# Cross-attention and quantized feed-forward: value-block loads issued in parts, some softmax-side work and the first key and query products in another order

## The reference

```python
q = (layernorm(x) @ Wq); k = context @ Wk; v = context @ Wv      # 8 heads of 64
attn = softmax(einsum('bhsd,bhld->bhsl', q, k) * scale)
x = x + (einsum('bhsl,bhld->bhsd', attn, v) -> rows) @ Wo + bo
xq = fake_quant(layernorm(x))        # one scale from the largest |value| of the whole tensor
h = fake_quant(silu(xq @ qw(w_gate).T) * (xq @ qw(w_up).T))     # again one scale for all of h
x = x + h @ qw(w_down).T
```

## Time and profile before

| | us |
|---|---|
| median of 3 runs | 533.98 (533.91 to 534.53) |
| the profiled execution | 534.28 |
| its span | 532.5 |
| TensorE busy in the span | 523.9 |
| VectorE busy | 448.7 |

### The profile page before, as it was taken

The page is one execution under the profiler, slowest core; times in us unless marked ns, Lnnn a source line. Parts: engine busy times, 40 slices in busy tenths (PEclk is TensorE's granted clock), DMA queues, the critical chain, the costliest instruction groups (busy, mean ns, idle before and its releaser), DMA issues.

```text
span 532.5 us, 7840 instructions
## 1 busy us (share of the span) xinstructions
PE 523.9 (98%) x2659; PEld 352.8 (66%) x2666; DVE 448.7 (84%) x808; ACT 288.9 (54%) x416; POOL 229.4 (43%) x347
## 2 busy tenths in 40 slices
PE   8999999999999999999999999999999999999997
PEld 8888788787888888888777644444444445444444
DVE  4968798989989899898899689998999988776663
ACT  4844645565465654554435745545554543999300
POOL 4397679688596886866454000000000000055332
PEclk9999999999999999999999999999999999999999
DMA  8946365846667566435959984842243021499997
GB/s 307 315 180 183 112 180 187 285 155 211 221 196 245 182 224 190 153 111 169 224 84 353 247 207 180 319 120 44 77 118 94 26 41 30 163 334 209 135 111 127
DMA packets 82941, 93.81 MB, mean 176 GB/s; under 512 B 47085, under 2 KB 50157, under 8 KB 82645
## 3 DMA queue, kind: packets, MB, share of 16 engines
q1 hardware_dynamic: 77877, 84.13, 51.5%
q0 software_dynamic: 4320, 7.87, 9.9%
q10 hardware_dynamic: 704, 1.31, 0.8%
HBM read 47.51 MB, written 37.78 MB: 160 GB/s over the span
## 4 chain that ended last, share of the span: by engine, by line
PE 91%; DVE 4%; DMA 2%; issue 1%; SPq 1%; ACT 1%; POOL 0%; DVEq 0%
PE SP L653 14%; PE QO L648 14%; PE SP L450 6%; PE QO L415 4%; PE QO L414 4%; PE QO L413 4%; PE SP L693 4%; PE PTP L693 4%; PE QO L693 4%; PE PTP L483 3%; PE WOP L523 2%; PE WOP L525 2%; PE WOP L524 2%; PE MI L525 2%; PE MI L523 2%; PE MI L524 2%
## 5 line engine op out<-in xcount | busy, mean ns | idle before, releaser
L1599 POOL DMA_DIRECT2D out<-n2b x30 | 28.0, 974 | 204.6 <-DVE n2b L1410 204.5
L936 ACT ACTIVATE sil<-QO,fsc 128x512 f32<-128x512 f32 x87 | 59.8, 687 | 72.2 <-PE QO L648 71.3
L648 PE MATMUL QO<-nT,wgu 128*128 128x512 bf16 x340 | 87.2, 379 | 0.0
L653 PE MATMUL SP<-nT,wgu 128*128 128x512 bf16 x340 | 87.2, 379 | 0.0
L1357 DVE SCALAR_TENSOR_TENSOR h<-SP,fsc,sil 128x512 f32<-128x512 f32 x87 | 65.3, 750 | 16.1 <-PE SP L653 14.1
L1492 POOL TENSOR_TENSOR PN<-P,rs 128x512 f32<-128x512 f32 x64 | 44.6, 719 | 41.6 <-DVE rs L1019 41.6
L1363 DVE TENSOR_REDUCE hmx<-h 128x1 f32<-128x512 f32 x88 | 59.9, 685 | 2.9
L653 PEld LDWEIGHTS SP<-nT,wgu 128*128 128x128 bf16 x340 | 33.3, 98 | 40.1
L648 PEld LDWEIGHTS QO<-nT,wgu 128*128 128x128 bf16 x340 | 33.3, 98 | 40.1
L758 ACT ACTIVATE P<-P,r 128x616 f32<-128x616 f32 x32 | 25.9, 811 | 52.6 <-DVE P L1010 52.6
L965 ACT ACTIVATE h<-h,g 128x1536 int8<-128x1536 f32 (+2 forms) x38 | 44.3, 1262 | 0.0
(11 more groups left out here) (256 smaller groups left out, 1199.7 us busy)
## 6 DMA issues: line engine op xcount, KB each, us to landing
xTr<-in_xT SPq DMA_DIRECT2D x8, 1024.0 KB, 7.2
xn<-in_x SPq DMA_DIRECT2D x32, 256.0 KB, 4.0
out<-x SPq DMA_DIRECT2D x32, 256.0 KB, 3.1
n_rows<-n SPq DMA_DIRECT2D x32, 256.0 KB, 2.9
n2b<-n_rows SPq DMA_DIRECT2D x32, 256.0 KB, 3.6
out<-n2b POOLq DMA_DIRECT2D x30, 256.0 KB, 5.6
h_spill<-h SPq DMA_DIRECT2D x2, 2816.0 KB, 8.6
h<-h_spill SPq DMA_DIRECT2D x6, 768.0 KB, 8.0
```

The source lines that it names most:

```text
L648: mm = e.matmul(QO[:, at:at + 512], wgu_v[:, k, cols(ic)], nT[:, b % 2, :, k, :], start=(k == 0), stop=(k == 3))
L653: mm = e.matmul(SP[:, at:at + 512], wgu_v[:, k, cols(NI + ic)], nT[:, b % 2, :, k, :], start=(k == 0), stop=(k == 3))
L936: e.activation(sil[:, n % SR, :], QO[:, (n % 2) * 512:(n % 2) * 512 + 512], ACT.Silu, scale=fsc[:, ic:ic + 1]).then_inc(silu, 1)
```

## The change

Four things are changed; every operation stays, and the arithmetic too.

- *The start.* The second chunks of keys and Wk are requested ahead of Wq. TensorE does `k_chunk(1)` before the sums of Wq; the eighth key bank's nine products stand together behind chunk 2 (`k_last`). The first two query products run side by side in two banks, 24 matmuls in a fixed order, each with a wait for the one half it needs. ScalarE alternates wqs and xTs halves with three key copies between; both query copies come ahead of the halves of Wv. The low half of Wk's third chunk moves from VectorE to GpSimd.
- *Behind the value products.* On ScalarE `PV_high` comes ahead of `normed` (block 1: of `w_round(2)`), and normed(22) behind PT_high(28). On VectorE `second_stats`/`second_aggr` of tile 4b-5 stand behind soft_sub; the statistics of tiles 5 and 6 are moved to two other places. `split_hi` stands ahead of `w_round(4b+1)`.
- *The requests.* `load_vb` is parted: the 4 large requests stay, of the 8 small ones 4 stand in the turn of tile 4b+1 and 4 in that of 4b+2, behind `store_n2`.
- *The end.* `load_n2(0)` is requested behind store_n2(25), three stores earlier; store_v(0) ahead of load_w(0).

```diff
@@ -370,42 +370,77 @@
...
+                if k < 2:
+                    w.wait_ge(wk_lo, k + 1)
+                else:
+                    w.wait_ge(wk_lo_pool, 1)
+                for m in range(7):
                     mm = k_part(m, k, 1)
                     if k == 2:
                         mm.then_inc(k_mm, 1)
+            def k_last():
+                w.wait_ge(wq_c, 4)
+                for k in range(3):
+                    for i in (0, 2, 1):
+                        mm = k_part(7, k, i)
+                mm.then_inc(k_mm, 1)
...
+                pairs = [q_pairs(0), q_pairs(1)]
+                banks = [qo_bank("q", 0, 0), qo_bank("q", 0, 1)]
+                def high(m, k):
+                    w.wait_ge(wq_hi, k + 1)
+                    w.wait_ge(xT_hi, k + 1)
+                    return e.matmul(banks[m], pairs[m][k][0], pairs[m][k][2], start=(k == 0), stop=False)
...
+                high(0, 0)
+                weight_low(0, 0)
+                input_low(0, 0)
+                high(0, 1)
+                w.wait_ge(K_act, 3)
+                w.wait_ge(K_dve, 1)
+                high(1, 0)
+                weight_low(1, 0)
+                input_low(1, 0)
+                high(1, 1)
+                for m in range(2):
+                    weight_low(m, 1)
+                for m in range(2):
+                    high(m, 2)
+                for m in range(2):
+                    input_low(m, 1)
+                for m in range(2):
+                    high(m, 3)
+                weight_low(0, 2)
+                input_low(0, 2)
+                weight_low(0, 3)
+                input_low(0, 3).then_inc(q_mm, 1)
+                weight_low(1, 2)
+                input_low(1, 2)
+                weight_low(1, 3)
+                input_low(1, 3).then_inc(q_mm, 1)
@@ -534,12 +569,13 @@
             k_chunk(0)
+            k_chunk(1)
             w.wait_ge(ws_sum, 3)
             e.matmul(WOP[:, :], ones[:, :], wsum[0], start=True, stop=True).then_inc(wq_sum, 1)
-            k_chunk(1)
             k_chunk(2)
+            k_last()
             q_first()
-            for m in range(1, 4):
+            for m in range(2, 4):
                 q_chunk(0, m)
@@ -789,28 +825,30 @@
             e.dma_start(wkr[:, 0, :], wk_v[0]).then_inc(ld_k[0], 16)
+            e.dma_start(wkr[:, 1, :], wk_v[1]).then_inc(ld_k[1], 16)
             e.dma_start(wqr[:, 2:4, :], wq_v[:, 2:4, :]).then_inc(ld_wq, 16)
-            e.dma_start(wkr[:, 1, :], wk_v[1]).then_inc(ld_k[1], 16)
             e.dma_start(wkr[:, 2, :], wk_v[2]).then_inc(ld_k[2], 16)
+                if k == 2:
+                    k_out(0, 0)
+                    k_out(0, 1)
+                    k_out(1, 0)
                 w.wait_ge(wq_c, k + 1)
                 copy(wqs[:, 0, k, :], wqr[:, k, :]).then_inc(wq_hi, 1)
-            for k in range(4):
                 split_hi(0, k)
-            k_out(0, 0)
-            k_out(0, 1)
-            for m in range(1, 8):
+            for m in range(2, 8):
                 k_out(m, 0)
+            q_copy(0, 0)
+            q_copy(0, 1)
             for k in range(3):
                 w.wait_ge(ld_wv, 16)
                 copy(wvs[:, 0, k, :], wvr[:, k, :]).then_inc(wv_hi, 1)
-            q_copy(0, 0)
+            q_copy(0, 2)
             w.wait_ge(ld_wo, 16)
             copy(wos[:, 0], wor[:, :, :]).then_inc(wo_hi, 1)
-            for m in range(1, 4):
-                q_copy(0, m)
+            q_copy(0, 3)
@@ -842,12 +880,13 @@
-            w_round(2)
             for b in range(1, 7):
                 s = 4 * b
+                PV_high(b - 1)
                 if b > 1:
                     normed(s - 6)
-                PV_high(b - 1)
+                else:
+                    w_round(2)
                 PT_high(s)
@@ -863,11 +902,11 @@
                 q_copy(b + 1, 3)
-                if s + 1 < 26:
-                    w_round(s + 1)
                 if b + 2 < NB:
                     for k in range(4):
                         split_hi(b + 2, k)
+                if s + 1 < 26:
+                    w_round(s + 1)
                 PT_high(s + 2)
@@ -877,9 +916,9 @@
                 normed(s - 3)
-            normed(22)
             PV_high(6)
             PT_high(28)
+            normed(22)
             soft_exp(29)
@@ -1100,23 +1141,24 @@
             split_k(0)
+            split_k(1)
             w.wait_ge(ld_wq, 32)
             e.tensor_tensor(wsum[0], wqr[:, 0, :], wqr[:, 1, :], ALU.add).then_inc(ws_sum, 1)
             e.tensor_tensor(wsum[1], wqr[:, 2, :], wqr[:, 3, :], ALU.add).then_inc(ws_sum, 1)
             w.wait_ge(ws_sum, 2)
             e.tensor_tensor(wsum[0], wsum[0], wsum[1], ALU.add).then_inc(ws_sum, 1)
-            split_k(1)
+            split_k(2)
             for k in range(4):
                 w.wait_ge(wq_sum, 1)
                 e.scalar_tensor_tensor(out=wqr[:, k, :], in0=WOP[:, :], scalar=-1.0 / D, in1=wqr[:, k, :],
                                        op0=ALU.mult, op1=ALU.add).then_inc(wq_c, 1)
-            split_k(2)
+            k_out(1)
             for k in range(3):
                 split_lo(0, k)
             w.wait_ge(wq_hi, 4)
             less(wqs[:, 1, 3, :], wqr[:, 3, :], wqs[:, 0, 3, :]).then_inc(wq_lo_dve, 1)
@@ -1170,6 +1212,8 @@
             soft_sub(4)
+            first_stats(5)
+            first_aggr(5)
@@ -1177,10 +1221,6 @@
             w_inverse(2)
-            first_stats(5)
-            first_aggr(5)
-            first_stats(6)
-            first_aggr(6)
@@ -1190,13 +1230,17 @@
                     residual(s - 5)
-                    second_stats(s - 5)
-                    second_aggr(s - 5)
                 PV_low(b - 1)
                 if b > 1:
                     largest(s - 7)
+                else:
+                    first_stats(6)
+                    first_aggr(6)
                 soft_max(s + 1)
                 soft_sub(s + 1)
+                if b > 1:
+                    second_stats(s - 5)
+                    second_aggr(s - 5)
                 PT_low(s)
@@ -1521,6 +1565,8 @@
+            w.wait_ge(wk_hi, 3)
+            less(wks[:, 1, 2, :], wkr[:, 2, :], wks[:, 0, 2, :]).then_inc(wk_lo_pool, 1)
@@ -1629,7 +1677,11 @@
-                for hh in range(H):
+            def load_vb_rest(b, h0, h1):
+                w.wait_ge(pv_mm, 4 * b)
+                for hh in range(h0, h1):
@@ -1677,8 +1729,8 @@
             e.dma_start(ctr[:, 0, :], ctx_v[0]).then_inc(ld_k[0], 16)
+            e.dma_start(ctr[:, 1, :], ctx_v[1]).then_inc(ld_k[1], 16)
             e.dma_start(wqr[:, 0:2, :], wq_v[:, 0:2, :]).then_inc(ld_wq, 16)
-            e.dma_start(ctr[:, 1, :], ctx_v[1]).then_inc(ld_k[1], 16)
             e.dma_start(ctr[:, 2, :], ctx_v[2]).then_inc(ld_k[2], 16)
@@ -1694,13 +1746,14 @@
                 load_xn(n)
+            store_v(0)
             load_w(0)
-            store_v(0)
             store_v(1)
             load_xT(2)
             store_v(2)
             load_w(1)
-            load_vb(0)
+            load_vb_main(0)
@@ -1717,23 +1770,27 @@
                     load_xn(s + 4)
-                load_vb(b)
+                load_vb_main(b)
                 store_w(s - 1)
+                load_w(s + 1)
                 for n in range(s + 1, s + 4):
-                    if n < 26:
-                        load_w(n)
                     store_x1(n - 5)
                     if n + 4 >= XR and n + 4 < NT:
                         load_xn(n + 4)
                     if n >= 6:
                         store_n2(n - 6)
+                    if n < s + 3:
+                        load_vb_rest(b, 4 * (n - s - 1), 4 * (n - s))
                     if n - 1 < 26:
                         store_w(n - 1)
+                    if n + 1 < min(s + 4, 26):
+                        load_w(n + 1)
             load_wgu(0)
             load_wgu(1)
@@ -1743,12 +1800,11 @@
             store_n2(25)
+            load_n2(0)
             store_n2(26)
             for n in range(28, NT):
                 store_n2(n - 1)
                 store_x1(n)
-                if n == 28:
-                    load_n2(0)
             store_n2(31)
```

More of the change, by code:

```diff
@@ L372, in k_chunk @@
                     k_part(m, k, 2)
-                if k == 2:
-                    w.wait_ge(wq_c, 4)
-                    for k0 in range(2):
-                        for i in (0, 2, 1):
-                            k_part(7, k0, i)
-                    k_part(7, 2, 0)
-                    k_part(7, 2, 2)
-                w.wait_ge(wk_lo, k + 1)
-                for m in range(8 if k == 2 else 7):
+                if k < 2:
[3 more added lines that the diff above has]
+                for m in range(7):
                     mm = k_part(m, k, 1)
@@ L1554, in gpsimd_program @@
             soft_norm(4)
+            first_scale(5)
+            first_bias(5)
             w_integer(2)
-            for n in (5, 6):
-                first_scale(n)
-            for n in (5, 6):
-                first_bias(n)
```

(8 more changed lines are left out.)

31 lines of the change are left out of this document (14 added, 17 removed).

## The result

The changed kernel takes 537.25 us (median of 11 executions, 535.25 to 541.22), the kernel before 533.98 (533.22 to 534.65). The ratio is 1.0068, 95% interval 1.0051 to 1.0085: 0.7% slower, and a microsecond above the top of the forecast's range. Two things are new: the time itself, and its spread, 6 us against 1.4. The profiled execution of the changed kernel took 535.84 (its span 534.1 against 532.5), so it is one of the shorter ones and shows only 1.6 us of the 3.3.

The account below looks back on a forecast made before the run. TensorE, busy 98%, bounds the kernel, so only its stops can give anything. 0.35 + 1.06 - 1.3 + 0.2 = 0.3 us gained, forecast 533.7 us; its own range 532.4 to 535.2, 8 in 10 531.2 to 536.3.

Parts of the forecast that it names:

- The start: Up to PT(0): 1.9 us gained at the third query product, 0.35 left because GpSimd's run holds PT(0).
- Block 1: Head of block 1: statistics of tiles 5 and 6 moved out of the way of the `os` halves, 1.06 us gained.
- Blocks 2 to 6: Heads of these blocks: four small requests make load_xn(4b+7) late; 1.3 us lost, from 2.1 to 0.7.
- The landing: Time from load_xn's issue to arrival, 2.8 to 4.1 us; named as what would make the forecast wrong above all.
- Block 7 and the end: From S(29) to L621, the sync queue deciding: 0.2 us gained, from -0.6 to 0.8.
- residual(28) would wait for store_x1(24): Sign at the end: store_x1(24) lands at 283.95, making residual(28) 0.45 us later.
- leaving it gives about nothing: Small requests' old place at the block's head: no engine waited behind it except VectorE, 0.2 us for a weight row.
- the loads land late: Rival: load_xn(4b+7) behind four small requests lands after 4.1 us at all heads; 2.6 us slower, 536.6; chance 0.24.
- The small requests hide: Rival: four small requests fit SP's idle time, no load is late; 3.3 us gained, 530.7; chance 0.18.

Follow-up runs that it names:

- the second profile: The changed kernel run again with nothing edited: median 537.17 us (534.94 to 540.58); the profiled execution took 538.50.
- the requests alone: Kernel before with only the requests' part: four small requests behind store_n2(4b-5), four behind store_n2(4b-4); 546.41 us, ratio 1.0246.
- 2, 4, 2: Kernel before with only the small requests respread: 2 at the block's head, 4 behind store_n2(4b-5), 2 behind store_n2(4b-4); 534.02 us, ratio 1.0003.
- 4, 4, 0: Changed kernel with 4 small requests at the block's head, 4 behind store_n2(4b-5), none in front of load_xn(4b+7); 531.00 us, ratio 0.9951.

## Why the prediction was wrong, step by step

The start of S and of the product of gcol (L657) in the first profile after, less the same in the profile before, gives each step's share: PT(4) -0.03, S(5) -1.09, S(9) +0.42, S(13) +0.71, S(17) +1.18, S(21) +1.66, S(25) +1.73, S(29) +2.12, L657 +1.46. So the forecast had 0.3 us gained up to L657, and 1.46 were lost.

- **The start**: forecast 0.35 us gained, measured 0.03 at PT(4) and 0.11 at PT(0). The reading was right: the third query product at 23.11 (forecast 23.05), the sum's matmul without a wait, GpSimd's run as the thing that holds PT(0). The gain is smaller because the run began 0.25 later than before, at 29.91: the statistics ahead of it started at 26.28, not at 26.0. The wait is 0.73 us and not 1.3, because TensorE lost 0.73 us more by start times at the value rows ahead of PT(0), 0.46 of it a wait that the profile lists. VectorE's split of block 1, placed in front of v_low(0), held them: it took 3.46 us where it had taken 1.47. In the trace of before it read:

```profile
33.34 1.47 DVE L973 TENSOR_TENSOR xTs<-xTr,xTs 128x512 fp32r<-128x512 f32 x1
```

  It began 1.7 us earlier now, and both times ended half a microsecond behind GpSimd's subtraction of Wo (34.27 before, 34.52 now): it does not run beside it. The Trainium skill, "SBUF — State Buffer", section "SBUF: two separate sides", says that a VectorE instruction with two SBUF inputs and a GpSimd instruction that reads SBUF exclude each other, and that the one that starts first has the shared port for its whole length. The trace agrees: 3.46 us for a split that began beside the 4.61 us of GpSimd, 0.68 for one of the same shape at 35.59, after it. The later moves confirm that GpSimd's run holds PT(0): with soft_norm(0) straight behind Wo's low half, PT(0) starts 1.5 us earlier.
- **Block 1**: forecast 1.06, measured 1.06 (S(5) 1.09 earlier, less 0.03 of the start). Right in place and size.
- **Blocks 2 to 6**: forecast 1.3 us lost, measured 2.82 (1.51, 0.29, 0.47, 0.48, 0.07). This is the step that failed: the term of 1.3 us for the four requests in front of load_xn(4b+7) was sized too small. The mechanism was the right one, each link of it: store_n2(0) on time, load_xn(11) behind four requests, VectorE waiting, S 3.59 us after the statistics (forecast 3.72). The first wrong term is the four requests' own time, put at 4 x 0.84 = 3.36 us from the ordinary spacing. In block 1 they took 4.43 in one profile and 4.36 in the other, since the third held the queue 1.91 and 1.83 us from start to start. In blocks 2 to 6 they took 3.34 or 3.35, as forecast. The maximum of the kind, 1.67 us for one request, stood in the earlier trace rows; I used the minimum and the step. That is the 1.1 us missing at b=2. The other heads came within 0.25 of their forecasts, all of them on the side of more loss.
- **The landing**, the second wrong term, and the larger one for the median. I took one value from each trace row of before and wrote of the time to landing that it "here is 2.8 to 4.1 us for the same load", but treated it as an uncertainty of the forecast and not as a cost. In the profile of before part of a later landing would have been absorbed: at four of the six heads the tile had landed 0.06 to 1.13 us before VectorE took it up, and at the other two VectorE was waiting. Once the load is late at all of them, each microsecond of landing goes through to TensorE but for the slack at b=6, and the median lies above what the shorter profile shows: the second profile's 2.66 us more lie almost wholly in these gaps. The first profile explains 1.6 us of the 3.3 lost, the second, of an execution above the median, 4.4 of 4.7 by its gaps. The clock comes on top, and it is not in either profile: the median execution itself, 537.25, had a mean clock of 0.997, an estimated 1.6 us by that number, where the first profile has 0.999. Whether a long wait lies ahead of it there, as in the run with the requests alone, is inferred, and so how the median's loss parts between gaps and clock stays open.
- **Block 7 and the end**: forecast 0.2 gained, measured 0.27 (S(29) 0.39 lost where half a microsecond was to be gained, 0.66 gained behind it). The queue did as foreseen: store_w(25) in step 252.67 (forecast 252.65; measured 254.40, less the 1.73 by which the block runs late), the first DMA_TRANSPOSE 0.94 later (forecast 0.95), load_xn(31) at 253.69 in step (forecast 253.6). It landed after 3.7 us instead of 2.7, the second wrong term again, which cost S(29) its gain; the end behind it gave more than was forecast, so that 0.27 agrees with 0.2 by luck. None of the transposes waited for n2b, and gcol starts 0.25 ahead of L657, where it started 0.89 ahead of L621 in the earlier trace rows. That residual(28) would wait for store_x1(24) is not seen: it starts without idle time.
- **What the sum left out**: of the place at the head, "leaving it gives about nothing". True of the kernel before (2, 4, 2 on it: 534.02), false of the changed one. With the work reordered and all eight at the head VectorE waits 8.4 us for weight rows; taking four away (4, 4, 0) gives 1.7 us of time. It did not falsify the forecast, since the change does take them away, but it hid that the two parts need each other, and that the good place was the first of the two new ones.

Of the rivals, "the loads land late" is the mechanism that happened, at the point it named (0.96 less 0.34 us of slack: before, row tile 11 landed 3.8 us ahead of PT(8), and the gap now opens at 3.1). That its 536.6 is so near 537.25 is partly luck. It took 4.1 us to landing at every head, where the first profile has 3.3 to 3.7; it lost 0.5 at the end, where 0.27 was gained; and it had neither the long third request nor the clock. I gave it 0.24 and the forecast 0.45, because two of four landings in one trace had been short. A wait that stands on a landing in each of four heads should have been priced at the longer ones. "The small requests hide" was wrong for four and right for two.

## What to carry to other kernels

Requests put in front of a load in a queue's idle time are free only up to that idle time and the slack behind it, and the threshold is sharp: here two cost nothing, three 0.8 us and four 6. Price them with the longest of their kind, and where a load becomes the last thing waited for, add its landing time's spread to the time, not to the error bar. When one part of a change reorders work, look anew at which loads it asks for earlier, because a place in the queue that was free may now be the bound.

## What the runs showed of the hardware

- The same 256 KB load, in the same place of the same program, landed after 3.3 us in one execution and 4.1 in another, and at the last head 3.7 and 4.9. With the requests alone the load of row tile 19 took 5.5 us, where it took 4.1 before.
- A small value request (6.5 KB) holds the sync queue for at least 0.78 us; singly up to 1.9 us from start to start, at the same place (the third in block 1) in both profiles of the changed kernel. A 256 KB store held it for 0.34 us in one execution and 1.58 in the other.
- After 3.56 us without a matmul TensorE was granted 0.50 of its clock for about 3.4 us; the clock fell 0.6 us after the matmuls had begun again. In the second profile of the changed kernel, whose longest wait at a head was 2.47 us, it did not fall.
- VectorE's 0.68 us subtraction on SBUF took 3.46 us when it began beside a 4.61 us subtraction of GpSimd.
